# TensorE's loop over the experts' tiles: eight tiles per round in place of four

## What is computed

```python
logits = einsum('nh,eh->ne', xt, router_w)            # 4096 tokens, 8 experts
scores, expert_idx = top_k(softmax(logits), 2)         # each token goes to two experts
h = einsum('nh,ehd->end', xt, up_proj)                 # 256 -> 2 * 256
hidden = silu(h[..., :256]) * h[..., 256:]
out_e = einsum('end,edh->enh', hidden, down_proj)      # 256 -> 256
out = einsum('ne,enh->nh', gate, out_e)
```

## Time and profile before

| | |
|---|---|
| median of 3 runs | 454.08 us (453.01 to 455.45) |
| the profiled execution's own time | 452.64 us |
| its span, first to last instruction | 450.8 us |
| TensorE (PE) busy | 383.5 us, 85% of the span |
| VectorE (DVE), ScalarE (ACT), GpSimd (POOL) busy | 273.9, 232.0, 215.8 us |
| share of PE in the chain of work that ended last | 57% |
| mean granted TensorE clock | 0.941 of full |

### The profile page before, as it was taken

How to read it: one execution, slowest core, us unless ns; L and a number is a source line. 1 busy time by engine, 2 the same in 40 slices (tenths; PEclk the granted TensorE clock), 3 DMA queues, 4 the chain that set the end, 5 groups by cost and what they waited for, 6 DMA issues and landing times.

```text
span 450.8 us, 8962 instructions
## 1 busy us (share of the span) xinstructions
PE 383.5 (85%) x2525; PEld 311.6 (69%) x2526; DVE 273.9 (61%) x774; ACT 232.0 (51%) x752; POOL 215.8 (48%) x213
## 2 busy tenths in 40 slices
PE   5489768688989944999999999999999998999860
PEld 1223758578988843788888888888888875666650
DVE  5799998346878733445444555445444534479984
ACT  1466745447687742444544545454545434566650
POOL 5252447666677671133333333333333332489983
PEclk9699889889999985899999999999999999999966
DMA  8752113334445322254443434343434323982222
GB/s 259 246 164 71 47 60 105 120 117 131 130 133 185 107 94 84 64 186 121 140 124 120 125 117 128 117 126 118 125 120 122 92 77 100 386 320 95 94 72 93
DMA packets 40434, 59.01 MB, mean 131 GB/s; under 512 B 6294, under 2 KB 27926, under 8 KB 40408
## 3 DMA queue, kind: packets, MB, share of 16 engines
q1 hardware_dynamic: 31712, 38.53, 28.5%
q0 software_dynamic: 6848, 18.70, 11.4%
q10 hardware_dynamic: 1848, 1.47, 1.1%
HBM read 35.79 MB, written 22.89 MB: 130 GB/s over the span
## 4 chain that ended last, share of the span: by engine, by line
PE 57%; DVE 12%; POOL 10%; issue 9%; ACT 5%; DMA 4%; SPq 1%; another core or an unknown queue 0%; POOLq 0%; DVEq 0%; ACTq 0%
PE bank L1104 15%; PE bank L1102 15%; PE bank L1103 14%; POOL xres L713 4%; PE bank L1228 3%; PE bank L1244 3%; POOL xres L706 3%; DMA xn<-x 3%; PE bank L1180 2%; DVE xn L782 2%; ACT junk L494 2%; DVE xst L760 2%; POOL slot_x L672 1%; POOL rstd L698 1%; DVE xT_l L790 1%
## 5 line engine op out<-in xcount | busy, mean ns | idle before, releaser
L687 POOL DMA_INDIRECT slot_y<-ey,dest x71 | 68.6, 966 | 138.2 <-ACT ey L547 108.4
L672 POOL DMA_INDIRECT slot_x<-xn,pos x64 | 66.4, 1038 | 34.9 <-PE bank L1104 15.2
L990 DVE TENSOR_TENSOR hid<-gact,bank 128x256 f32<-128x256 f32 x71 | 29.9, 421 | 78.2 <-ACT gact L531 52.4
L1102 PE MATMUL bank<-ew,exT_h 128*128 x142 | 63.6, 448 | 5.3 <-issue 4.5
L531 ACT ACTIVATE gact<-bank 128x256 f32<-128x256 f32 x71 | 27.4, 386 | 65.7 <-PE bank L1104 65.7
L1104 PE MATMUL bank<-ew,exT_l 128*128 x142 | 56.8, 400 | 0.0
L1103 PE MATMUL bank<-ew,exT_h 128*128 x142 | 56.8, 400 | 0.0
L1103 PE MATMUL bank<-w_l,xT_h 128*128 128x256 f32 x192 | 55.6, 290 | 1.3 <-issue 1.3
L1104 PE MATMUL bank<-w_h,xT_l 128*128 128x256 f32 x192 | 55.6, 290 | 0.2 <-issue 0.2
L1102 PE MATMUL bank<-w_h,xT_h 128*128 128x256 f32 x192 | 55.5, 289 | 0.1
L494 ACT ACTIVATE junk<-bank 128x256 bf16<-128x256 f32 x96 | 35.8, 384 | 37.2 <-PE bank L1104 37.2
(11 more groups left out here) (193 smaller groups left out, 960.9 us busy)
## 6 DMA issues: line engine op xcount, KB each, us to landing
ex<-slot_x SPq DMA_DIRECT2D x71, 129.0 KB
y_tok<-slot_y SPq DMA_DIRECT2D x8, 1024.0 KB, 13.9
ew_f<-experts SPq DMA_DIRECT2D x24, 256.0 KB
xres<-x SPq DMA_DIRECT2D x16, 256.0 KB
out<-xres SPq DMA_DIRECT2D x16, 256.0 KB, 2.1
xn<-x SPq DMA_DIRECT2D x6, 512.0 KB, 11.7
slot_y<-ey,dest POOLq DMA_INDIRECT x71, 2.4
xn<-x SPq DMA_DIRECT2D x4, 256.0 KB, 3.9
```

What stands on the lines that cost most here:

```text
L672: pool.indirect_dma_start(slot_x, bass.IndirectOffsetOnAxis(ap=pos[:, k, t:t + 1], axis=0), xn[:, t, :], None).then_inc(s["scattered"], 16)
L687: pool.indirect_dma_start(slot_y, bass.IndirectOffsetOnAxis(ap=dest[:, m % 4:m % 4 + 1], axis=0), ey[:, m % 4, :], None).then_inc(y_out[m ...
L990: v.tensor_tensor(hid[:, m % 2, :], gact[:, m % 2, :], h_ps[m % 2][:, F:2 * F], ALU.mult).then_inc(s["hid_done"], 1)
L1102: mm(dst, a_h, b_h, start=first, stop=False)
```

## The change

TensorE's loop over the experts' tiles makes eight tiles per round, in 8 rounds in place of 16. At the head of each round it reads ten owners in place of eight: the eight of the round's tiles and the two of the tiles before, whose `down_proj` comes two tiles late. The same 64 tiles are done in the loop, in the same order, with the same semaphores and thresholds. The four tiles ahead of the loop and the three behind it are as they were, and so are the programs of the other engines.

```diff
-            with pe.Fori(1, QUADS) as i:
-                w8 = experts_of(i * 4 - 4, 8)
-                for u in range(4):
-                    expert(i * 4 + u, 4 + u, i, w8[4 + u], w8[2 + u])
+            with pe.Fori(0, (QUADS - 1) // 2) as i:
+                w10 = experts_of(i * 8 + 2, 10)
+                for u in range(8):
+                    expert(i * 8 + (4 + u), 4 + u, i * 2 + (1 + u // 4), w10[2 + u], w10[u])
```

## The result

The changed kernel is slower: 474.19 us, median of 6 runs (472.68 to 475.99), against 454.56 (452.10 to 455.74) for the kernel before, run beside it. The ratio is 1.044, 95% interval 1.040 to 1.048. The forecast was 450.7, with a range of 449.0 to 454.8.

The account below looks back on a forecast made before the run. TensorE was taken to set the experts' stage's time, losing it at loop heads. Heads removed -4.0, two more owners +0.3 and register arithmetic +0.3 gave -3.4 us: 454.08 to 450.7 us, range 449.0 to 454.8.

Parts of the forecast that it names:

- Two more owners at the 8 heads that stay: Owners' load at each remaining loop head: 35 ns more for two owners, 0.3 us in all, bounds 0 to 1.2.
- the second rival: Load of ten owners is dear: 455.2 us if made as two, 454.4 if like the tail's; 6% for both.
- A fall of the clock ... I give it no chance of its own: Clock falling through denser work in the experts' stage: would look like 454.1 us; no chance of its own.
- The eight heads removed: Eight of 16 loop heads go, at 0.50 us each: 4.0 us less.
- The lead of 0.4 us: In every tile TensorE's sequencer is some 0.4 us ahead after stopping for `hidT_l`; this doesn't grow from tile to tile.
- the rival of the needed rests: Other work keeps pace only because TensorE pauses every fourth tile, so pauses return as waits: 454.1 us; 8%.
- Register arithmetic: Round number times 8 and times 2 at the loop heads: 0 to 0.5 us over 8 heads, taken as 0.3.
- The rival of the blocks: Longer loop body leaves instruction memory, so each of 7 branches back waits for a fetch: 458.9 us; 6%.
- The tail's head: Behind the loop, its load of seven owners (1492 ns) and 0.78 us of "issue" stay unchanged.
- 8 of them of about 630 ns: Sign in the changed profile: `TENSOR_LOAD` 10 times in all, 8 of about 630 ns.
- the rounds of 20.9 us: Sign in the changed profile: rounds of 8 x 2.545 + 0.57, that is 20.9 us.
- the heads' 0.50 us: Excess at each loop head reached by the branch back: the mean round of 10.683 us less 4 x 2.545.

Follow-up runs that it names:

- e5: The kernel before plus owner loads of many sizes and starts, values used, behind its last work: 551.07 us, one run, no result as a time.
- e8: The kernel before, its eight owners per head loaded from place 4i - 2 instead of 4i - 4: 495.69 us, against 454.69 for the kernel before.
- e3: The changed kernel with twenty matmuls that nothing reads ahead of each head's load: 470.13 us, ratio 1.041.
- e2: The changed kernel with twelve owners loaded from 8i instead of ten from 8i + 2: 450.23 us, ratio 0.994 to the kernel before.
- e7: The kernel before, each head loading ten owners from 4i - 4 and using eight: 460.4 us, against 454.69 for the kernel before.
- e4: The changed kernel with its ten owners in two loads, two from 8i + 2 and eight from 8i + 4: 455.54 us, ratio 1.007.
- e11: The changed kernel, owners read by aligned loads of eight at the head and four inside the second tile: 439.14 us, ratio 0.990 to the kernel before.
- e10: Eight-tile rounds cut between turn_ex and down_proj, owners in three loads of four: 436.64 us, ratio 0.987 to the kernel before.
- e6: The kernel before, its four-tile rounds cut inside a tile, between turn_ex and down_proj: 451.3 us, ratio 0.994.
- e9: Four-tile rounds cut between turn_ex and down_proj, owners in two loads of four, the second a tile later: 437.13 us, ratio 0.985 to the kernel before.

## Why the prediction was wrong

**The step that failed is "Two more owners at the 8 heads that stay".** It priced two owners at 35 ns, 0.3 us in all, 1.2 at most. They cost 2.04 us a head, 16.3 in all. The slope came from two rows, four owners at 0.52 and eight at 0.59. Both are whole groups of four from multiples of four, and the change is the first load whose start is not a multiple of four: `i * 8 + 2`. e5 and e8 show that the start does it: by the law above ten from a multiple of four would have cost 0.5 us more than eight, ten from two past one cost 2.0: 0.5 for the two owners more, 1.3 for the start, and 0.24 that only the working loop shows and that is open. The step extended a line along one variable, the number, past the point where a second one, the start, changed with it. Even as a slope it was poor: in e5 the load of four takes 0.34 and not 0.52, which was measured in another stage, so a group of four more costs 0.25, not 0.07. (One reading of the prediction was off by a slice, without effect: PE's row has its 9s from slice 17 to 33, and slice 34 has an 8.)

**The row that spoke against it was on the page.** The tail's seven owners took 1.49 us. The prediction called this row "not in line", and gave it to the second rival as an accident or a property of unknown kind, with 0.5 us a head. Seven owners are one group and three left over: it was the one row that was not whole groups. Read as a property, 1.49 - 0.52 = 0.97 us for three owners is 0.3 for each one read singly, and ten read singly come to 3 us, an estimate in hindsight; the measured load is 2.64. The row is not wholly explained even now: by e5's rule seven owners take 1.06 us, and the tail's load of seven took 1.23 to 1.55 in the other runs. With that rival's 6% and 0.5 us a head, its direction was right and its size wrong by four.

The Trainium skill has a price of this size in "Runtime: NRT & Kernel Launch", section "Instruction fetch mechanics", the very section that the prediction cited for something else: a register load takes about 200 ns per register, even for bulk. For ten that is an estimate of 2.0 us; the trace agrees for owners read singly (0.23 us each in e5) and not for aligned groups of four, where e5 has 0.065 per owner. By the same figure the load of eight would have taken 1.6 us, and the earlier trace rows had 0.59, so it could warn of the size but not say when it holds. The Trainium skill's "DMA: Bandwidth & Descriptors", section "Latency and other measured facts", has a floor of about 600 ns for a `tensor_load`; e5's 343 ns for four is below it.

**"A fall of the clock ... I give it no chance of its own" failed as well, 9.3 us.** I asked for a fall from denser work. It came from the opposite, a pause of 2.3 us, and e3, which fills the pause, takes it away. It hangs wholly on the first failure: with pauses of 0.7 us at most (e2), 0.8 (e7) and 1.2 (e4) there is none. Together the two terms are 25.6 us against the 0.3 of the sum.

**What held.** The eight heads removed are worth 4.0 us: e11, which differs from the change only in its loads, gains 4.3, ratio 0.990 (0.987 to 0.993). The lead of 0.4 us holds in tiles 5 to 8: in round 2 of the changed kernel `down_proj`'s first address stands 0.42 to 0.44 us ahead of its weights in tiles 2 to 8 alike, and the tiles begin 2.55 us apart. From round 2 on no wait on `hidT_l` or `ex` appeared, in e10 and e11 neither, where the array hardly rests, so the rival of the needed rests is out there. In the first round it is not: e6, e9, e10 and e11 wait once for `ex`, 0.7 to 1.1 us. e11's small wait on `exT_l` is in the place of "issue", of the same 0.27 us, and so no new cost. Register arithmetic, put at 0.3 us, cost nothing: FUSED_REGOPS is 68 ns and the branch 215, as before. The rival of the blocks is out by q8. The load is one instruction and not two, and its count, 10, is as forecast. The tail's head shows 0.78 us again. Of the marks that it set, the trace denies two at first sight: "8 of them of about 630 ns", and the rounds of 20.9 us, which are 22.9 (24.5 where the clock falls).

**One cause of the heads' 0.50 us was better named than used.** The prediction showed that the sequencer's lead at the cut is too short, and took it for fixed. e6 and e9 show that it depends on where the round is cut and on the longest single load: moved and with loads of four, the heads of the loop are hidden, all in e10 and nearly all in e9, and 6.6 us are gained (e9) where the change could have gained 4.0 at best.

## What to carry to other kernels

When an index expression of a register load changes, price the load by its start and its remainder, not by its count: on this chip round the window out to whole groups of four from multiples of four, even where that reads values that nobody uses (twelve took 0.85 us, ten of them 2.64). A row that does not fit the line drawn through two others must be explained before the line is used beyond them. Before making a loop's heads fewer, try to hide them: cut the round where the sequencer is furthest ahead of the array and split what the head must read, and check that no pause on the array grows long enough for the clock to pay for it too.

## What the runs showed of the hardware

- A sequencer's load of n values of a list in SBUF, by e5: 0.085 + 0.255 us per aligned group of four, 0.24 per value left over; from an unaligned start about 0.08 + 0.23 per value. Unexplained: 0.24 more for unaligned starts in the working loop (the changed kernel, e8), 0.23 for e4's second load, and 0.3 to 0.5 for four loads at fixed places in e5.
- A pause of the array of 2.1 to 2.3 us in a stage otherwise at 98% busy was followed by 3.4 us at 1.2 GHz after six of eight heads (the entry among them), one of 1.8 us after ten of sixteen (e8), one of 1.2 us after none of seven (e4), and those of 0.8 us and less after none (e2, e3, e7). Once the clock fell behind two pauses of 1.06 and 0.94 us that lay 0.4 us apart (e6). The price was 1.4 to 1.6 us each time, on top of the pause. Why some pauses of the same length are followed by a fall and others not stays open.
- A loop body of eight tiles on TensorE is branched back to without an instruction fetch.
